# Cross-attention readout: the pass over the context's low part as two 64-row matmuls, with the high exponentials copied to the upper rows

## What is computed

```python
def xattn(hidden, memory, mask):             # hidden = layernorm(x), memory = ctx [8, 64, 1024]
    scores = einsum('bsd,bmd->bsm', hidden, memory) / sqrt(D)
    scores = where(mask[:, None, :], scores, -1e30)
    attn = softmax(scores, axis=-1)
    return einsum('bsm,bmd->bsd', attn, memory)          # the "readout"

x = x + xattn(layernorm(x), ctx, mask)
y = layernorm(x)
base = y @ weight.T
w_dense = top-2 of softmax(y @ router_w.T), made to sum to 1
x = x + base + 2.0 * einsum('nd,erd,ne,eor->no', y, lora_A, w_dense, lora_B)
```

## Time and profile before

| | us |
|---|---|
| median of 3 runs | 1054.68 (1054.35 to 1054.80) |
| the profiled execution, its own time | 1054.39 |
| its span, first to last instruction | 1052.3 |
| TensorE matmul busy | 1043.5 (99%), 6078 matmuls |
| TensorE weight load busy | 1028.7 (98%) |
| DVE busy | 817.3 (78%) |
| ACT busy | 477.7 (45%) |
| POOL busy | 147.8 (14%) |
| chain that ended last, share on TensorE | 95% |

### The profile page before, as it was taken

The page is one execution under the profiler, slowest core; times in us unless marked ns, Lnnn a source line. Parts: engine busy times, 40 slices in busy tenths (PEclk is TensorE's granted clock), DMA queues, the critical chain, the costliest instruction groups (busy, mean ns, idle before and its releaser), DMA issues.

```text
span 1052.3 us, 18830 instructions
## 1 busy us (share of the span) xinstructions
PE 1043.5 (99%) x6078; PEld 1028.7 (98%) x6078; DVE 817.3 (78%) x2203; ACT 477.7 (45%) x929; POOL 147.8 (14%) x278
## 2 busy tenths in 40 slices
PE   8999999999999999999999999999999999999998
PEld 7999999999999999999999999999999999999998
DVE  6987887788777887878877888778888778777663
ACT  7754544445434544444444345344444444443320
POOL 3211211111111111111111111111111111111100
PEclk9999999999999999999999999999999999999999
DMA  8555556654556555475545655455654565554431
GB/s 306 201 160 124 149 154 163 170 147 122 149 158 179 143 123 142 143 201 131 152 115 150 185 149 150 135 132 171 163 150 137 118 174 153 152 149 114 114 75 58
DMA packets 157248, 156.81 MB, mean 149 GB/s; under 512 B 95120, under 2 KB 130064, under 8 KB 157200
## 3 DMA queue, kind: packets, MB, share of 16 engines
q1 hardware_dynamic: 156336, 154.82, 53.9%
q10 hardware_dynamic: 864, 1.45, 0.4%
HBM read 78.74 MB, written 33.55 MB: 107 GB/s over the span
## 4 chain that ended last, share of the span: by engine, by line
PE 95%; DVE 2%; DMA 1%; POOL 0%; issue 0%; ACT 0%; SPq 0%; ACTq 0%; DVEq 0%; POOLq 0%
PE base_ps L1086 28%; PE base_ps L1088 28%; PE base_ps L1087 28%; PE ro_ps L1150 3%; PE s_ps L1114 3%; PE ro_ps L1151 3%; PE s_ps L1113 3%; DMA xT_raw<-in_xT 1%; DVE stats L885 0%; DVE w_lo L331 0%; DVE x_first L879 0%; SPq L374 0%; DVE xT_lo L801 0%; DMA w_raw<-w_raw 0%; SPq L410 0%
## 5 line engine op out<-in xcount | busy, mean ns | idle before, releaser
L1086 PE MATMUL base_ps<-w_hi,xT_hi 128*128 128x388 f32 x1512 | 513.7, 340 | 0.0
L1088 PE MATMUL base_ps<-w_hi,xT_lo 128*128 128x388 f32 x1512 | 512.5, 339 | 0.0
L1087 PE MATMUL base_ps<-w_lo,xT_hi 128*128 128x388 f32 x1512 | 511.4, 338 | 0.0
L1087 PEld LDWEIGHTS base_ps<-w_lo,xT_hi 128*128 128x128 f32 x1512 | 284.7, 188 | 2.8
L1086 PEld LDWEIGHTS base_ps<-w_hi,xT_hi 128*128 128x128 f32 x1512 | 284.0, 188 | 2.7
L1088 PEld LDWEIGHTS base_ps<-w_hi,xT_lo 128*128 128x128 f32 x1512 | 284.3, 188 | 0.0
L487 POOL TENSOR_TENSOR rstd<-var_eps,neg_half 128x1 f32<-128x1 f32 x64 | 65.3, 1020 | 567.7 <-DVE var_eps L892 567.7
L901 DVE STREAM_TRANSPOSE x2T<-xq 128x512 f32<-128x512 f32 x122 | 121.5, 1072 | 5.3 <-DMA xq<-xn 4.7
L605 ACT CAST xT_hi<-x2T 128x512 fp32r<-128x512 f32 x122 | 69.6, 618 | 85.3 <-DVE x2T L901 85.3
L916 DVE MAX8 top<-base_ps 128x8 f32<-128x8 f32 x64 | 11.2, 174 | 106.8 <-PE base_ps L1088 106.8
L599 ACT ACTIVATE xn<-w_raw,shift,rstd 128x1024 f32<-128x1024 f32 x32 | 39.9, 1245 | 94.1 <-POOL shift L490 94.1
(11 more groups left out here) (128 smaller groups left out, 1382.5 us busy)
## 6 DMA issues: line engine op xcount, KB each, us to landing
xT_raw<-in_xT SPq DMA_DIRECT2D x62, 512.0 KB, 5.3
xq<-xn SPq DMA_DIRECT2D x244, 128.0 KB, 3.6
w_raw<-in_x SPq DMA_DIRECT2D x32, 512.0 KB, 3.5
out<-x_first SPq DMA_DIRECT2D x32, 512.0 KB, 2.7
out<-w_raw SPq DMA_DIRECT2D x31, 512.0 KB, 2.7
x_first<-in_x SPq DMA_DIRECT2D x30, 512.0 KB, 3.5
h<-w_raw SPq DMA_DIRECT2D x248, 16.0 KB, 1.9
w_raw<-w_raw SPq DMA_DIRECT2D x120, 32.0 KB, 1.9
```

Of the source, the lines that this page charges most:

```text
L1086: pe.matmul(out_, a_hi, w_h, start=start, stop=False, skip_group_check=again)
L1087: pe.matmul(out_, a_hi, w_l, start=False, stop=False, skip_group_check=again)
L1088: return pe.matmul(out_, a_lo, w_h, start=False, stop=stop, skip_group_check=again)
```

## The change

The readout keeps its two 128-row matmuls over `ctx_hi`, now one after the other. The two over `ctx_lo` become 64-row matmuls: half 0 takes rows 0 to 63 of `eT` and of `ctx_lo`, half 1 takes rows 64 to 127 of a new tile `eT_up` and of `ctx_lo`. Both take the high exponentials only, so the product of the low exponentials with the low context is left out of the sum. For this the high exponentials have to stand in rows 0 to 63 of `eT`, so the layout of `e_split` changes (`e_part`, `by_keys`, `first_e`), and that of the context rows on the host with it. ACT makes one more copy for each tile, of the 64 upper halves' rows into `eT_up`, right behind the cast to `eT`. TensorE waits for the first copy ahead of its first matmul and for the second ahead of its second. The two increments of `readout_done` are now those of the third and the fourth matmul. The centred context is written in place over `ctxT_raw`, and SP waits for `ctxT_split` in place of `ctx_centred` ahead of the next load into it.

```diff
@@ -127,7 +127,6 @@
         ctx_raw = sb("ctx_raw", [P, CW])
         mask_raw = ctx_raw[:, D:CW].bitcast(u8)
         ctxT_raw = sb("ctxT_raw", [P, C, M])
-        ctxT_centred = sb("ctxT_centred", [P, C, M])
         ctx_sum = sb("ctx_sum", [P, M])
         mask_f = sb("mask_f", [P, M])
         mask_bias = sb("mask_bias", [P, M])
@@ -170,6 +169,7 @@
         e_inv = sb("e_inv", [P, 1])
         e_scale = sb("e_scale", [P, 1])
         eT = sb("eT", [P, P], f32r)
+        eT_up = sb("eT_up", [P, P], f32r)
         top8 = sb("top8", [P, 8])
         top8_at = sb("top8_at", [P, 8], u32)
         top2_at = sb("top2_at", [P, 2])
@@ -224,7 +224,14 @@
 
         def first_e(i):
 
-            return e_split[:, :].rearrange("p (r j) -> p j r", j=Q)[:, 2 * i:2 * i + 2, :]
+            return e_split[:, :].rearrange("p (l r j) -> p l j r", l=2, j=Q)[:, i]
+
+        def e_part(i):
+
+            return e_split[:, :].rearrange("p (j l r) -> p l j r", l=2, j=Q)[:, i]
+
+        def by_keys(t):
+            return t.rearrange("p (j r) -> p j r", j=Q)
 
         def by_blocks(t):
             return t.rearrange("p (j r) -> p j r", r=QP)
@@ -445,7 +452,7 @@
                     sp.wait_ge(ctx_split, b + 1)
                     sp.wait_ge(mask_step, b * 3 + 3)
                     load_ctx(b + 1)
-                    sp.wait_ge(ctx_centred, b + 1)
+                    sp.wait_ge(ctxT_split, b + 1)
                     load_ctxT(b + 1)
 
             for j in range(TPB):
@@ -525,7 +532,7 @@
         def _(act):
             def ctxT_high(b):
                 act.wait_ge(ctx_centred, b + 1)
-                act.copy(ctxT[:, :, 0:M], ctxT_centred[:, :, :]).then_inc(ctxT_hi_done, 1)
+                act.copy(ctxT[:, :, 0:M], ctxT_raw[:, :, :]).then_inc(ctxT_hi_done, 1)
 
             def ctx_high(b):
                 act.wait_ge(ctx_loaded, b * 16 + 16)
@@ -572,12 +579,13 @@
                 act.wait_ge(eq_done, count(tile, 1, -4))
                 act.activation(e_all[:, :], s_all[:, :], ACT.Exp, bias=neg_max[:, :],
                                accum_out=e_sum[:, :]).then_inc(exp_done, 1)
-                act.activation(e_split[:, 0:M], s_all[:, :], ACT.Exp, bias=neg_max[:, :]).then_inc(exp_done, 1)
+                act.activation(e_part(0), by_keys(s_all[:, :]), ACT.Exp, bias=neg_max[:, :]).then_inc(exp_done, 1)
 
             def eT_copy(tile):
                 act.wait_ge(e_loaded, count(tile, 16 * Q, 16 * Q * (1 - 4)))
                 act.wait_ge(readout_done, count(tile, 2))
                 act.copy(eT[:, :], e_raw).then_inc(eT_copied, 1)
+                act.copy(eT_up[M:P, :], e_raw[0:M, :]).then_inc(eT_copied, 1)
 
             def first_softmax_exp(tile):
                 act.wait_ge(softmax_step, count(tile, 5, 3))
@@ -586,12 +594,13 @@
                 act.wait_ge(eT_done, count(tile, 1))
                 act.activation(e_all[:, :], s_all[:, :], ACT.Exp, bias=neg_max[:, :],
                                accum_out=e_sum[:, :]).then_inc(exp_done, 1)
-                act.activation(first_e(0), by_blocks(s_all[:, :]), ACT.Exp, bias=neg_max[:, :]).then_inc(exp_done, 1)
+                act.activation(first_e(0), by_keys(s_all[:, :]), ACT.Exp, bias=neg_max[:, :]).then_inc(exp_done, 1)
 
             def first_eT_copy(tile):
                 act.wait_ge(eT_done, count(tile, 1, 1))
                 act.wait_ge(readout_done, count(tile, 2))
                 act.copy(eT[:, :], et_ps).then_inc(eT_copied, 1)
+                act.copy(eT_up[M:P, :], et_ps[0:M, :]).then_inc(eT_copied, 1)
 
             def norm2(tile):
                 act.wait_ge(shift2_done, count(tile, 1, 1))
@@ -764,13 +773,13 @@
 
             def ctx_centre(b):
                 dve.wait_ge(ctx_mean_done, b + 1)
-                dve.tensor_tensor(ctxT_centred[:, :, :], ctxT_raw[:, :, :],
+                dve.tensor_tensor(ctxT_raw[:, :, :], ctxT_raw[:, :, :],
                                   h_ps[:, P:P + M].unsqueeze(1).to_broadcast([P, C, M]),
                                   ALU.subtract).then_inc(ctx_centred, 1)
 
             def ctxT_low(b):
                 dve.wait_ge(ctxT_hi_done, b + 1)
-                dve.tensor_tensor(ctxT[:, :, M:2 * M], ctxT_centred[:, :, :], ctxT[:, :, 0:M].bitcast(f32),
+                dve.tensor_tensor(ctxT[:, :, M:2 * M], ctxT_raw[:, :, :], ctxT[:, :, 0:M].bitcast(f32),
                                   ALU.subtract).then_inc(ctxT_split, 1)
 
             def first_norm1_stats():
@@ -847,7 +856,7 @@
 
             def softmax_split(tile):
                 dve.wait_ge(exp_done, count(tile, 2, 2))
-                dve.tensor_tensor(e_split[:, M:2 * M], e_all[:, :], e_split[:, 0:M].bitcast(f32),
+                dve.tensor_tensor(e_part(1), by_keys(e_all[:, :]), e_part(0).bitcast(f32),
                                   ALU.subtract).then_inc(e_split_done, 1)
                 softmax_sum(tile)
 
@@ -862,7 +871,7 @@
 
             def first_softmax_split(tile):
                 dve.wait_ge(exp_done, count(tile, 2, 2))
-                dve.tensor_tensor(first_e(1), by_blocks(e_all[:, :]), first_e(0).bitcast(f32),
+                dve.tensor_tensor(first_e(1), by_keys(e_all[:, :]), first_e(0).bitcast(f32),
                                   ALU.subtract).then_inc(e_split_done, 1)
                 softmax_sum(tile)
 
@@ -1143,12 +1152,15 @@
                 first = isinstance(b, int) and tile == (0, 0)
                 if j % TPB == 0 and not first:
                     pe.wait_ge(ctx_split, b + j // TPB + 1)
-                pe.wait_ge(eT_copied, count(tile, 1, 1))
                 for i in range(2):
-                    if first:
-                        pe.wait_ge(first_ctx_half if i == 0 else ctx_split, 1)
+                    pe.wait_ge(eT_copied, count(tile, 2, i + 1))
                     pe.matmul(half(ro_ps, i), eT[:, :], half(ctx_hi, i), start=True, stop=False)
-                    pe.matmul(half(ro_ps, i), eT[:, :], half(ctx_lo, i), start=False, stop=True)\
+                if first:
+                    pe.wait_ge(first_ctx_half, 1)
+                    pe.wait_ge(ctx_split, 1)
+                for i, e in enumerate([eT, eT_up]):
+                    rows = slice(i * M, (i + 1) * M)
+                    pe.matmul(half(ro_ps, i), e[rows, :], half(ctx_lo, i)[rows, :], start=False, stop=True)\
                       .then_inc(readout_done, 1)
 
             def base(tile, g, chunks_):
@@ -1329,7 +1341,7 @@
         "x": np.ascontiguousarray(x.reshape(B * S // P, P, D)),
         "xT": np.stack([by_contraction(rows if i < 4 else by_fourths(rows))
                         for i, rows in enumerate(x.reshape(B * S // P, P, D))]),
-        "ctx": np.concatenate([np.stack([by_blocks(np.concatenate([rows, rows])) for rows in ctx]), mask_words], axis=2),
+        "ctx": np.concatenate([np.stack([np.concatenate([by_blocks(rows)] * 2) for rows in ctx]), mask_words], axis=2),
         "ctxT": np.stack([by_contraction(rows) for rows in ctx]),
         "wT": by_quadrants(np.concatenate([weight[:w0], lora_a.reshape(E * R, D), router, weight[w0:]])),
         "bT": by_blocks(lora_b.transpose(0, 2, 1).reshape(E * R, O)),
```

## The result

The changed kernel is slower: 1066.36 us in the median (1065.99 to 1068.4), against 1054.67 us of the kernel before on the same chip. The ratio is 1.0115 with a 95% interval of 1.0103 to 1.0128, which is 10.9 to 13.5 us lost; the two medians lie 11.7 us apart, and that is the figure I use. The forecast was 1048.1 us with a range of 1040 to 1066; the time lies just beyond the upper end, on the other side of no change.

What follows compares the result with a forecast made beforehand. TensorE's queue was taken as the bound, time being the sum of distances between its starts: 1054.39 - 7.6 + 1.0 = 1047.8 us, plus 0.29 from profiled run to median, 1048.1 us; range 1040 to 1066.

Steps and rivals of the forecast that it cites:

- What a pass costs: TensorE's readout: each 512-column pass takes 0.231 us, the mean distance between starts, so four take 0.924 us a tile.
- TensorE loads one set ahead: Readout's 64-row matmuls: the second waits 0.11 us for its weight load, so the gain is 0.119 us a tile, 7.6 us.
- Changing between full and half height: TensorE, into and out of the 64-row matmuls: bounded at 0 to 0.27 us a change, 0 to 35 us in all; taken as 0.
- Rival 2: Readout: each change of height stops the pipeline with an exposed load; 1061.7 us, or 1082 if the array empties; chance 0.28.
- the stagger: Readout: the second 64-row matmul starts 0.11 us after the first, so the pair takes 0.34 us in place of 0.46.
- the emptying: Array at each change of height: the matmul in flight must leave first, adding 0.16 us a change, 20.5 us in all.
- point of decision: Cost of one change of height from which the slower outcome decides: 0.06 us, where it eats the 0.119 us gain.
- The copy and the readouts with little room: ACT's copy to eT_up: hidden except at 17 readouts at j = 4 or 6, each waiting 0 to 0.1 us; 1.0 us taken.
- Edits with one answer: Exponentials' write in four blocks, centring in place, SP's other wait, host layout: cost 0; the write without cover 0.1 us a tile.
- The granted clock is 1.00 in every slice: TensorE's clock: at the upper of its two levels, 2.4 GHz, throughout, so no clock effect is to be won.

Runs made afterwards that it cites:

- the second pair: Changed kernel with the pair of 64-row matmuls issued twice in a row in each tile: 1080.99 us, ratio 1.0248, 14.6 us above the changed kernel.
- the serial pair: Changed kernel with both 64-row matmuls on rows 0 to 63 of eT, in the same half of the array: 1079.64 us, ratio 1.0236.
- the kernel at 1055.23 us: Changed kernel with its low pass again as two 128-row matmuls of eT, all else of the change kept: 1055.23 us, ratio 1.0004.
- 128-column probe: Kernel before plus one 128-column matmul a tile ahead of the readout, over rows 0 to 63 only: 1083.26 us; over all 128 rows: 1062.72 us.

## Why the prediction was wrong

The bound and the sum were right: TensorE's queue sets the time, and the loss is the sum of distances between its starts. With the measured sizes the same sum gives, for a tile, -0.231 + 2 x 0.195 = +0.159 us, times 64 = 10.2, and with the 0.6 of the other parts 10.8 of the 11.7 us measured.

- *What a pass costs, 0.231 us a tile.* Right: 14.6 us for the second pair, and 13.3 us between the overlapped and the serial pair.
- *TensorE loads one set ahead, so the second half-height matmul starts 0.11 us late.* Wrong. The two loads start together and so do the matmuls; the gain of the overlap was 0.231 us a tile and not 0.119. The earlier trace rows show one set ahead for loads that use all rows; they can't tell what loads of different halves do. This error alone would have made the forecast too high by 7.2 us. What the Trainium skill says in TensorE: Matmul & The Clock Gate, Part 3, that such matmuls start some 4 ns apart, agrees with the traces: here they are within 0.01 us.
- *Changing between full and half height: I take 0.* This is the step that failed. I bounded a change by 0 and 0.27 us and took the lower end, with the argument that no load in the steady part is held back. But no row of the steady part contained a change, so that row could not be near it. It is 0.195 us, 128 times: 25 us against the forecast. The Trainium skill says in TensorEngine Tiling (Array Packing), Tiling Modes, that a change of mode drains TensorE. The traces agree as far as they go: 0.09 us pass between the end of the stream and the next load. Whether the array itself is empty by then, the profile does not show.
- *Rival 2* had the right mechanism and was put at 1061.7 or, with emptying, at 1082 us. It carried the stagger that did not exist (+7.2 us) and either none of the emptying or 0.16 us for it, where 0.09 was measured. The first of the two came within 4.7 us of the time by two errors that in part cancel, which is luck: a stagger of 0.11 us too much, and emptying of twice 0.09 us too little. With the pair starting together its point of decision would have been 0.115 us a change, half of a pass.
- *The copy and the readouts with little room: 1.0 us of waits.* The kernel with the low pass at full height gives 0.6 us for all of that together, with an interval from -0.6 to 1.4 us. The places were other ones than said. The prediction priced 17 readouts with a room of mostly 0.34 to 0.41 us at up to 0.1 us each. Three of the 17 had next to none already (0.05 us behind the casts at 69.06 and 389.80, 0.11 behind the one at 133.35). It is these three and the first readout of all where the copy delays a matmul, 0.25 us together; at the other 14 it delays none. The second copy ends 0.32 us behind the cast, not 0.25. The chain in the earlier trace rows did move: DVE waits for the readout for 28.8 us in all in that kernel, 12.2 before, since half 0 is done a pass later.
- *Edits with one answer.* They hold together: layout, centring in place and SP's other wait are all in the kernel at 1055.23 us; none was tried alone.
- *The granted clock is 1.00 in every slice.* Not in the first: the matmuls of the kernel before stand 0.21 us apart up to 6.3 us. This changes no term of the sum.

The expected gain did not go off the critical path, and it was not lost to contention. It was made, 14.8 us, and paid back 1.7 times over at the two ends of each pair. With this price one shared pass a visit loses, at any size: a pair saves 0.231 us and the visit costs 0.39. By an estimate from the measured sizes, a visit that replaces four passes by two pairs would save 0.462 and so gain 0.07 us a tile; this readout has only one product with 64 rows, so it was not tried.

## What to carry to other kernels

A pair of 64-row matmuls in the two halves of the array is worth one pass, but count the changes of height on either side of it, 0.195 us each here, with 128 columns and with 512: gather all work of one height between two changes, and do it only where it saves more than 0.39 us. A bound that no row of the profile touches is not at its cheap end because the rows show no trouble; where a cost has no instance in the profile, take the middle of the bounds or the nearest exposed load, and make a probe of one small matmul first. And when TensorE is 99% busy before and after, look at the weight loads' idle time and at durations that grow by one load (0.49 for 0.39): that is where a stopped stream shows.

## What the runs showed of the hardware

- A change between 128-row and 64-row matmuls costs 0.195 us around a 128-column probe, 0.196 with 512 columns by the medians of the runs, and 0.197 to 0.201 by the timelines, into 64 rows and out of them alike. It is 0.09 to 0.10 us until a load starts, and 0.105 us for the load, which in none of these timelines starts ahead of the change.
- 64-row matmuls in different halves and banks start within 0.01 us of each other, and so do their weight loads (512.39, 512.39). The loads of a following pair are made ahead of it, 0.11 us behind those of the first (615.72 and 615.61).
- 64-row matmuls in the same half go one after the other, at 0.21 us a tile by the time of the runs and 0.228 by the timelines.
- A matmul with 64 stationary columns and all 128 rows caused no stop: 1062.99 us against 1062.72 with 128 columns.
- TensorE starts at the matmul distance of the lower clock and changes to that of the upper one at a time that differs between executions: 128-column matmuls go from 0.21 to 0.11 us apart at 6.4 us in the profile before, and behind 16 us in that of the changed kernel.
